# Attention masks written into the score banks by ScalarE instead of added by mask matmuls, in a gated cross-attention and mixture kernel

## The reference, cut to what matters

```python
scores = jnp.einsum('bhnd,bhmd->bhnm', Q, K) / jnp.sqrt(jnp.float32(D))
scores = jnp.where(mask == 0, -jnp.inf, scores)          # L0: mask (1, 1, 256, 77), per query and key
attn = jax.nn.softmax(scores, axis=-1)
...
scores = jnp.where(key_padding_mask[:, None, None, :], -jnp.inf, scores)   # L1: mask (16, 77), per batch and key
```

## Time and profile before

| what | value |
|---|---|
| median of three runs | 1448.2 us |
| the profiled execution: time, span | 1449.66 us, 1447.9 us |
| mean granted TensorE clock | 0.947 of 2.4 GHz |
| mask matmuls, line 632 | 256 of 9188 matmuls |
| score products of the same units | 768 matmuls of 312 columns |
| stage 0, first to last mask matmul | 22.4 to 296.5 us |
| stage 1, first to last mask matmul | 727.8 to 1016.6 us |

### The profile page before, as it was taken

How to read it: one execution, slowest core, us unless ns; L and a number is a source line. 1 busy time by engine, 2 the same in 40 slices (tenths; PEclk the granted TensorE clock), 3 DMA queues, 4 the chain that set the end, 5 groups by cost and what they waited for, 6 DMA issues and landing times.

```text
span 1447.9 us, 27923 instructions
## 1 busy us (share of the span) xinstructions
PE 1310.0 (90%) x9188; PEld 1215.8 (84%) x9189; DVE 940.3 (65%) x2018; ACT 570.5 (39%) x1000; POOL 804.7 (56%) x927
## 2 busy tenths in 40 slices
PE   6999999979796999999269999999689999799998
PEld 5999999969796888888269999999578888788887
DVE  5777777768753333333246777777596877978886
ACT  2334443322232444444123344434334445344543
POOL 6555555528475111111678999995145554577775
PEclk9999999985798999999569999999899999999999
DMA  3222222232122333332332333330200000000000
GB/s 84 70 68 68 67 67 68 58 93 59 57 105 97 94 88 87 87 87 66 66 56 41 46 46 46 46 50 10 102 1 1 0 0 0 1 16 23 29 22 29
DMA packets 108363, 76.07 MB, mean 53 GB/s; under 512 B 49914, under 2 KB 100886, under 8 KB 108054
## 3 DMA queue, kind: packets, MB, share of 16 engines
q1 hardware_dynamic: 93408, 54.99, 14.2%
q0 software_dynamic: 12288, 16.82, 5.9%
q10 hardware_dynamic: 2614, 3.57, 0.8%
HBM read 40.94 MB, written 31.53 MB: 50 GB/s over the span
## 4 chain that ended last, share of the span: by engine, by line
PE 77%; DVE 9%; POOL 5%; issue 4%; ACT 2%; DMA 2%; ACTq 0%; DVEq 0%; POOLq 0%; SPq 0%
PE PSUM L578 14%; PE PSUM L580 14%; PE PSUM L579 14%; PE PSUM L655 10%; PE PSUM L641 5%; PE PSUM L632 3%; PE PSUM L1365 2%; PE PSUM L1354 1%; PE PSUM L1444 1%; PE PSUM L2157 1%; PE PSUM L2138 1%; PE PSUM L2139 1%; PE PSUM L2149 1%; POOL s_x L783 1%; DVE s_t_xn L2043 1%
## 5 line engine op out<-in xcount | busy, mean ns | idle before, releaser
L542 ACT ACTIVATE s_a_prob_t<-PSUM 128x640 f32<-128x640 f32 x128 | 89.8, 702 | 218.6 <-PE PSUM L641 218.6
L655 PEld LDWEIGHTS PSUM<-s_a_v_diagonal,s_a_prob_t 128*128 128x128 f32 x1280 | 157.5, 192 | 18.7 <-issue 14.1
L655 PE MATMUL PSUM<-s_a_v_diagonal,s_a_prob_t 128*128 128x54 f32 (+2 forms) x1280 | 162.9, 276 | 9.7 <-ACT s_a_prob_t L542 4.4
L1608 POOL TENSOR_TENSOR s_f_h_lo<-s_f_h,s_f_h_hi 128x512 fp32r<-128x512 f32 x64 | 89.2, 1402 | 111.0 <-ACT s_f_h_hi L1575 111.0
L1090 POOL TENSOR_TENSOR s_m_x_hi<-s_m_bias,s_ones 128x128 fp32r<-128x128 f32 x72 | 28.7, 400 | 195.3 <-PE PSUM L1463 186.5
L535 ACT ACTIVATE s_a_prob<-s_a_prob 128x624 f32<-128x624 f32 x128 | 92.2, 721 | 99.9 <-DVE s_a_prob L418 99.9
L1328 DVE TENSOR_TENSOR s_m_h<-PSUM,s_m_h 128x256 f32<-128x256 f32 x72 | 30.6, 425 | 140.6 <-ACT s_m_h L1134 140.6
L783 POOL DMA_INDIRECT s_x<-sorted_y,s_a_slot x64 | 101.9, 1592 | 22.4 <-issue 9.9
L411 DVE TENSOR_REDUCE s_a_row_max<-PSUM 128x8 f32<-128x624 f32 x128 | 102.3, 799 | 7.9 <-PE PSUM L632 5.9
L418 DVE TENSOR_TENSOR s_a_prob<-PSUM,s_a_row_max 128x624 f32<-128x624 f32 x128 | 103.1, 805 | 5.5
L641 PE MATMUL PSUM<-s_ident,s_a_prob 128*128 128x128 f32 x640 | 96.8, 283 | 2.9 <-ACT s_a_prob L535 2.9
(11 more groups left out here) (300 smaller groups left out, 4520.7 us busy)
## 6 DMA issues: line engine op xcount, KB each, us to landing
s_m_xn<-sorted_x SPq DMA_DIRECT2D x12, 771.0 KB, 5.5
sorted_y<-s_m_xn SPq DMA_DIRECT2D x12, 768.0 KB, 6.9
sorted_x<-s_zeros SPq DMA_DIRECT2D x16, 514.0 KB, 4.2
s_x<-x SPq DMA_DIRECT2D x16, 256.0 KB, 3.4
s_moe_raw<-moe_w SPq DMA_DIRECT2D x16, 256.0 KB, 3.3
y<-s_x SPq DMA_DIRECT2D x16, 256.0 KB, 2.1
s_late_raw<-moe_w SPq DMA_DIRECT2D x11, 256.0 KB, 2.7
s_a_ctx<-ctx SPq DMA_DIRECT2D x32, 78.0 KB, 2.7
```

Of the source, the lines that this page charges most:

```text
L542: act.activation(a.prob_t[j % 2][:], a.prob_t_ps, ACT.Copy).then_inc(a.pt_done, 1)
L655: last = pe.matmul(a.o_ps[:, first:first + heads, :], a.prob_t[j % 2][:, c, :], a.v_diagonal[b.z][:, j // BT, at:at + heads * VW].rearrang ...
L1608: pool.tensor_tensor(f.h_lo[m % 4][:], f.h[m % 4][:], f.h_hi[m % 4][:].bitcast(F32), ALU.subtract).then_inc(f.h_split, 1)
```

## The change

The mask matmuls go. ScalarE copies the mask, broadcast over the heads, into both banks of a unit before the score products, and the products are issued without a start flag, so that they add onto it. TensorE waits for `masked` in place of `scores_read`. At the start of each stage four matmuls with a start flag (`open_scores`) touch all columns of the score banks. The masks are now plain f32, and stage 1's is no longer divided by 128. ScalarE's new instructions stand at fixed places of its list.

```diff
--- before.py
+++ after.py
@@ -40,7 +40,6 @@
 EARLY_CHUNKS = BATCH
 LATE_CHUNKS = 3 * (EXPERTS + 1) - EARLY_CHUNKS
 BIAS_ROWS = 2 * (EXPERTS + 1)
-KEY_ROW = 1.0 / P
 CHOICES = 4
 SORTED = 2 * TILES + EXPERTS
 GROUP = 6
@@ -251,6 +250,7 @@
             k_rounded = sem("a_k_rounded")
             k_residue = sem("a_k_residue")
             kd_done = sem("a_kd_done")
+            masked = sem("a_masked")
             scores_ps = sem("a_scores_ps")
             max_done = sem("a_max_done")
             scores_read = sem("a_scores_read")
@@ -314,15 +314,14 @@
                 self.o_lo = sb(scope, n + "o_lo", [P, KC, SEQ], F32R)
                 if stage == 0:
                     self.mask_raw = sb(scope, n + "mask_raw", [P, BT, CTXP])
-                    self.mask = sb(scope, n + "mask", [P, BT, CTXP], F32R)
-                    self.ident = sb(scope, n + "ident", [P, P], F32R)
+                    self.mask = sb(scope, n + "mask", [P, BT, CTXP])
                 else:
                     self.slot = [sb(scope, n + f"slot{z}", [P, BT, 2], U32) for z in two]
                     self.mask_u8 = sb(scope, n + "mask_u8", [P, BATCH, CTX], U8)
 
                     late_sums = sums[:, TILES // 2:, :].rearrange("p t c -> p (t c)")
                     self.mask_raw = late_sums[:, 0:BATCH * CTXP].rearrange("p (b n) -> p b n", n=CTXP)
-                    self.mask = sb(scope, n + "mask", [P, BATCH, CTXP], F32R)
+                    self.mask = sb(scope, n + "mask", [P, BATCH, CTXP])
                 self.scores = PSUM[:, 0:4, :].rearrange("p (b c) n -> p b c n", b=2)
                 self.prob_t_ps = PSUM[:, 4:6, :].rearrange("p c (h n) -> p (c h) n", n=P)[:, 0:PC]
                 self.o_ps = PSUM[:, 6, 0:HPC * VW].rearrange("p (h n) -> p h n", n=VW)
@@ -535,6 +534,15 @@
                 act.activation(a.prob[j % 2], a.prob[j % 2], ACT.Exp,
                                scale=HD ** -0.5).then_inc(a.exp_done, 1)
 
+            def mask_laid(b, j):
+
+                if a.stage == 0:
+                    mask = a.mask[:, j % BT, :].unsqueeze(1)
+                else:
+                    mask = a.mask[:, bass.ds(b.n, 1), :]
+                act.activation(a.scores[:, j % 2, :, 0:HPC // 2 * CTXP].rearrange("p c (h n) -> p c h n", n=CTXP),
+                               mask.unsqueeze(1).broadcast_to([P, 2, HPC // 2, CTXP]), ACT.Copy).then_inc(a.masked, 1)
+
             def transposed(b, j):
                 u = UNITS * b.count + j
                 act.wait_ge(a.pt_ps, u + 1)
@@ -547,14 +555,19 @@
 
             act.wait_ge(consts_done, 1)
             x_rounded(Block(0, 0, 0, a.base))
+            act.wait_ge(a.mask_done, a.stage + 1)
+            for j in range(2):
+                mask_laid(Block(0, 0, 0, a.base), j)
             q_rounded(Block(0, 0, 0, a.base))
 
             def body(b, behind, ahead):
                 if behind:
                     transposed(b.last(), 3)
                 exponential(b, 0)
+                mask_laid(b, 2)
                 transposed(b, 0)
                 exponential(b, 1)
+                mask_laid(b, 3)
                 if ahead:
                     x_rounded(b.next())
                 transposed(b, 1)
@@ -562,8 +575,11 @@
                     o_rounded(b.last())
                 exponential(b, 2)
                 if ahead:
+                    mask_laid(b.next(), 0)
                     q_rounded(b.next())
                 exponential(b, 3)
+                if ahead:
+                    mask_laid(b.next(), 1)
                 transposed(b, 2)
 
             paired_blocks(act, BATCH, body, a.base)
@@ -617,20 +633,14 @@
                 m, qt = j // BT, j % BT
                 pe.wait_ge(a.kd_done, b.count + 1)
                 pe.wait_ge(a.q_split, b.count + 1)
-                after(pe, a.scores_read, u - 1)
+                pe.wait_ge(a.masked, u + 1)
                 q_hi = a.q_hi[b.z][:, m, qt * P:(qt + 1) * P]
                 q_lo = a.q_lo[b.z][:, m, qt * P:(qt + 1) * P]
                 for c in range(2):
                     heads = slice(c * HPC // 2, (c + 1) * HPC // 2)
                     ps = a.scores[:, j % 2, c, 0:HPC // 2 * CTXP].rearrange("p (h n) -> p h n", n=CTXP)
-                    product(pe, ps, [(q_hi, q_lo, a.kd_hi[b.z][:, m, heads, :], a.kd_lo[b.z][:, m, heads, :])],
-                            stop=False)
-                    if a.stage == 0:
-                        lhs, mask = a.ident[:], a.mask[:, qt, :].unsqueeze(1)
-                    else:
-                        lhs, mask = ones_r[:], a.mask[:, bass.ds(b.n, 1), :]
-                    last = pe.matmul(ps, lhs, mask.broadcast_to([mask.shape[0], HPC // 2, CTXP]),
-                                     start=False, stop=True)
+                    last = product(pe, ps, [(q_hi, q_lo, a.kd_hi[b.z][:, m, heads, :], a.kd_lo[b.z][:, m, heads, :])],
+                                   start=False)
                 last.then_inc(a.scores_ps, 1)
 
             def transpose_prob(b, j):
@@ -680,17 +690,25 @@
                     last = pe.matmul(ps, ones_r[:], a.bias_parts[:], start=False, stop=True)
                 last.then_inc(a.y_ps, 1)
 
+            def open_scores():
+
+                for z in range(2):
+                    for c in range(2):
+                        ps = a.scores[:, z, c, 0:HPC // 2 * CTXP].rearrange("p (h n) -> p h n", n=CTXP)
+                        pe.matmul(ps, ones_r[:], ones_r[:, 0:CTXP].unsqueeze(1).broadcast_to([P, HPC // 2, CTXP]),
+                                  start=True, stop=True)
+
             first = Block(0, 0, 0, a.base)
             if a.stage == 0:
                 pe.wait_ge(pool_const, 9)
+            pe.wait_ge(consts_done, 1)
+            open_scores()
             pe.wait_ge(a.w_split, 4 * a.stage + 2)
             keys_values(first)
             transpose_x(first)
             pe.wait_ge(a.w_split, 4 * (a.stage + 1))
             queries(first)
-            pe.wait_ge(consts_done, 1)
             pe.wait_ge(a.y_done, a.base + 1)
-            pe.wait_ge(a.mask_done, a.stage + 1)
             pe.wait_ge(a.v_ones, 2 + 3 * a.stage)
 
             def body(b, behind, ahead):
@@ -2398,7 +2416,7 @@
         @block.vector
         def _(dve):
             dve.wait_ge(pool_const, 9)
-            dve.tensor_copy(a0.ident[:], ident[:]).then_inc(a0.y_done, 1)
+            dve.memset(a0.rstd[:], 1.0).then_inc(a0.y_done, 1)
 
             def mask_of_queries():
                 dve.wait_ge(a0.mask_in, 16)
@@ -2413,7 +2431,7 @@
                 dve.wait_ge(a1.v_ones, 3)
                 dve.tensor_copy(a1.mask_raw[:, :, 0:CTX], a1.mask_u8[:]).then_inc(a1.mask_cast, 1)
                 dve.wait_ge(a1.mask_cast, 1)
-                dve.tensor_scalar(a1.mask[:], a1.mask_raw, MASKED * KEY_ROW, None, ALU.mult).then_inc(a1.mask_done, 1)
+                dve.tensor_scalar(a1.mask[:], a1.mask_raw, MASKED, None, ALU.mult).then_inc(a1.mask_done, 1)
 
             attention_on_vector(dve, a1, z_sum, mask_of_keys, lambda: ffn_first_stats_on_vector(dve, f),
                                 lambda: ffn_first_norm_on_vector(dve, f))
```

## The result

The changed kernel took 1478.81 us (median; 1478.15 to 1482.72), the kernel before 1449.05 beside it: ratio 1.0209, 95% interval 1.0191 to 1.0228. The prediction was 1475, range 1450 to 1500, slower. The profiled execution's span is 1476.6 us, 28.7 above the one before.

A forecast was written before the change was run, and what follows sets the result against it. The prediction took a hand-over chain between ScalarE, VectorE and TensorE as the bound: three copies in it lengthen a block by 0.96 us, over 28 blocks 26.9 us, ends 0, giving 1475 us, range 1450 to 1500.

The forecast's parts named there:

- The price m: ScalarE's queue: how much later the next instruction starts after a mask copy; taken 0.62 us, with 0.50 and 0.78 kept.
- Unit 2's copy free: Behind exponential 0, the copy lies in ScalarE's 3.5 us of idle and costs nothing.
- Step 1: Score 1 loses its two mask matmuls, so less_max 1 and exponential 1 come 0.29 us earlier.
- Step 2: Unit 3's mask ahead of x_rounded delays normalise 0; transpose_o shifts +0.03 us, TensorE waits 0.9 us.
- Step 3: The mask of the next block's unit 0 stands ahead of q_rounded, which shifts by +0.34 us.
- Step 4: Next unit 1's mask precedes the copy of transposed probabilities 2, adding 0.62 us; weigh_values 2 shifts 0.96 in all.
- The ends: First and last blocks of each stage: between -1.2 and +1 us each, taken as 0.
- Throughput: Rival: TensorE's 17.7 of 17.8 us bounds a block, copies hide in ScalarE's idle; 1426 us, chance 0.10.
- the even case: Rival: the chain's slacks are larger by 0.9 us per block in all; 1448 within 3 us, chance 0.04.
- the slow write: Rival: ScalarE's write into PSUM beside other engines costs 0.9 us or more; 1498 us, chance 0.06.
- the clock: Rival: TensorE's stops bring half-rate spells of some 1.2 us in each block; 1509 us, chance 0.06.
- the first rival: Throughput decides: stage 0 saves 18.6 us, stage 1 is held at GpSimd's 17.9 us per block; chance 0.10.

The follow-up runs named there:

- no_mask_2: Changed kernel without the mask copy for unit 2 of each block, that unit's masking left out: 1478.72 us.
- move_all_keep: Changed kernel with three mask copies per block moved later on ScalarE and stage 1's query keeping moved from GpSimd to ScalarE: 1434.04 us, again 1435.87.
- no_masks: Changed kernel with every mask left out, neither copies nor mask matmuls: 1443.46 us.
- the position experiments: Changed kernel with one mask copy moved behind the critical ScalarE instruction it preceded: next unit 0's 1471.88 us, next unit 1's 1456.66, unit 3's 1459.65.
- before_copies: Kernel before, mask matmuls kept, plus three spare ScalarE copies of 128x624 per block into unused SBUF at the chain's three places: 1484.38 us.
- move_all: Changed kernel with three of four mask copies per block moved behind x_rounded, q_rounded and the copy of transposed probabilities 2: 1442.42 us, again 1442.19.

## Why the prediction was right, step by step

- *The price m.* Taken 0.62, measured 0.61 to 0.62. The Trainium skill ("Perfetto Trace Analysis", Optimizing Scalar/DVE Operations) gives ScalarE less access time on PSUM than on SBUF. The trace agrees for the duration, 0.68 to 0.69 us against 0.71 for the same copy into SBUF. It does not for the distance to the next instruction, which is what m is: 0.613 to 0.615 us (medians) into PSUM, 0.613 to 0.616 into SBUF. The 3.4 us that the prediction worked out from the page did not come.
- *Unit 2's copy free.* Shown by the 2.60 us of idle behind it and by no_mask_2.
- *Step 1, score 1 shorter by 0.29.* From weigh_values 2 to exponential 1: 234.55 - 227.40 = 7.15, before 7.44. Right.
- *Step 2, transpose_o at +0.03.* It starts 238.31 - 227.40 = 10.91 after weigh_values 2, before 10.98: -0.07. The hand-over from VectorE took 0.06 us, not 0.15, so the slack had been larger by 0.09. TensorE waits 0.51 us there and not 0.9, because it had already waited 0.25 at 235.19, ahead of weigh_values 0, for the normalise of the unit before (the code waits for `o_done` there, and block after block of stage 0 it starts 0.24 us behind that normalise). I had not seen that wait; it shifts nothing.
- *Step 3, q_rounded at +0.34.* 240.72 - 227.40 = 13.32, before 13.05: +0.27, 0.07 less than forecast. transpose_o came 0.10 us earlier than forecast, its record after the stop is 0.06 longer (0.66 for 0.60), and the rest is rounding and a slightly smaller m.
- *Step 4, +0.62 at weigh_values 2.* From q_rounded to the copy, 226.59 - 222.01 = 4.58 (the start of q_rounded one block earlier is 222.01), before 3.96: +0.62, and the hand-over is the same. Together 0.89, against 0.96 forecast.
- *The ends.* Taken as nothing, this is the term that was mis-sized: beyond 28 x 0.89 = 24.9 the span grew by 3.8 us. The last blocks of the two stages, at the 1.2 GHz level for part of their time, account for 3.1; the 1.3 and 0.4 ahead of the first o_rounded for 1.7; against them stands 1.0, since the fourteenth distance of each stage grew by 0.4 and not by 0.89. Why the changed kernel had that spell and the one before not is open; two profiles of move_all_keep have it in different stages.
- *The sum.* 24.9 + 3.8 = 28.7, against 26.9. The block was forecast 2.0 us too long over 28 blocks and the ends 3.8 too short: two errors of opposite sign, so the total is nearer than its terms by some luck. The mechanism does not hang on it.
- *Rivals.* Throughput is refuted by no_masks and by the position experiments; the even case and the slow write by the result and by m; the clock by 1.00 in the block, though a short form of it, 1.5 us in each last block, did come. The range from 1450 up also leaves out half of the even case (1448 within 3), which the prediction does not say. The part of the first rival that came true is GpSimd's limit in stage 1.
- *TensorE's busy time.* I forecast 16.3 us a block and it shows 17.14, since the recorded ends of matmuls fill part of each stop. Here the busy time understates the standing time. The 16.3 did not fit its own terms either: 18.8 less two waits of 0.9 is 17.0.

## What to carry to other kernels

An engine that is half idle can still be full at a place: look for what stands right behind an inserted instruction, and compare the stretch of idle ahead of that one with the price of the insertion. Put filler work behind the hand-over that the next engine waits for, not ahead of it; here that alone turned +2.1% into -0.5%. When a chain is shortened, the next limit may be an engine whose repeat was already equal to the period (GpSimd, 17.9 against 17.8 us), and relieving it pays only then.

## What the runs showed of the hardware beyond that

- ScalarE's copy of 128x624 f32 took 0.673 to 0.690 us from SBUF to PSUM and 0.704 to 0.716 into SBUF (before_copies); the next instruction started 0.61 to 0.62 us later in both cases.
- The start is where the clock makes executions differ, those of one kernel too (48.8 and 53.8 us for move_all). At 0.50 to 0.66 of the clock from 40 to 50 us the first o_rounded came at 55.9 us or later, at 1.00 at 51.2 or earlier. What decides it was not settled.
- The last block of a stage took 10.1 us, 10.5 once, or 11.6 with part of it at the 1.2 GHz level, after the same stop of 1.50 us (before and after). Stops of 0.5 and 0.9 us in every block of the changed kernel left the clock at 1.00.
